# A four-layer decoder on one core: unread products of TensorE while outputs are fetched, masked heads' keys made in head mixing, loads between stores in the paged attention

## The chip, the core and the metric

The kernel runs on one core of a Trainium2 chip: TensorE (PE) for matrix products, VectorE (DVE), ScalarE (ACT) and GpSimd (POOL) for the rest, and SyncE (SP) that issues most transfers. The metric is the device time of one execution in microseconds (us). The granted clock of TensorE is told as a share of its full 2.4 GHz: 1.00 is 2.4 GHz and 0.50 is 1.2 GHz.

## What is computed

x has 2 x 1024 tokens of width 256. Twelve sublayers follow each other, each as `x = layernorm(x + f(x))`. Those that the change touches, cut to what matters:

```python
# L0_attn: heads of one token attend to each other (16 heads of 16)
kv = (x @ Wdown + bdown) @ Wup + bup                   # latent of 64
att = softmax(einsum('bthd,btgd->bthg', rope(q), rope(k)) / 4)
x = layernorm(x + einsum('bthg,btgd->bthd', att, v) @ Wout + bout)
# L0_xattn: 16 masked heads over a context of 77 rows
k, v = ctx @ Wk.T + bk, ctx @ Wv.T + bv
scores = where(mask == 0, -1e9, q @ k.T / 4)
x = layernorm(x + softmax(scores) @ v @ Wo.T + bo)
# L0_ffn: a gated FFN with ternary weights and 8-bit rows
# L1_attn: attention by pages of 64 rows, 16 heads of 16
k = rope((x @ w_down) @ wk_up)
scores = where(page(key) <= page(query), q @ k.T / 4, min)
# L1_ffn: 8 experts, the one with the highest score;  L2_ffn: 8 experts, two of them, with a capacity
x = layernorm(x + sum_over_choices(gate * expert(x)))
```

The others are a context attention (L1_xattn), a gated linear attention (L2_attn), a self-attention on the context (L2_xattn), a causal linear attention (L3_attn), L3_xattn and a quantized FFN (L3_ffn).

## The kernel before

Each sublayer is a stage, a function with one program for each engine; the engines agree by semaphores. x stays in SBUF twice, token-major (`x_tok`) and turned (`xT`), in 16 tiles of 128 tokens. The order on each engine is the order in which the program is written.

**Head mixing** (`head_mixing_stage`, line 593). SP loads x in pieces of 512 tokens (`CW`), then the next stage's weights (`early`). PE makes for each 512 tokens the latents (L675, `latents`), and for each tile the queries (L683, L686) and the keys and values (L690, `front`). DVE multiplies each query head with each key head (L805; half of it is on POOL, L870), sums (L814), weighs the values (L824) and norms (L833). PE sums the weighted values (L697, `mix`), turns them (L707) and projects (L715). `k` counts steps over the tiles; in step k PE works on `mix(k - 1)`, then `turn`, `front(k + 3)`, `project` and the layer norm's turned tiles (`tail.turn`, L3034). POOL adds the output bias to x in four pieces (L880). PE's first wait is for the weights (`loaded`), ACT's too; ACT's first Activation is behind the first latents.

**Masked heads** (`masked_heads_stage`, line 890). PE first makes K and V of the 77 context rows (L944, L948), DVE makes from them `kz` (L1085), `v` (L1088) and from the mask `fill` (L1090, L1092). Then, for each tile: queries (L959), ACT's copy `qT` (L1041), scores (L970), on DVE the masked scores (L1101), their maximum (L1104), the difference (L1106) and the sum (L1112). POOL adds the bias to x at the start (L1134).

**Paged attention** (`paged_attention_stage`, line 150). Queries and keys are split in bf16 parts; a part goes to DRAM and from there to the stacks Q and K of three slots. For each of the two sequences b there are four rounds r (r = 0, 1 the queries of two groups of heads, r = 2, 3 the keys). A round ends in ACT's casts (L274, L276), POOL's differences (L311, L314), DVE's L298, L300 and L304, and SP's store of two DMAs (L224). ACT may write the parts of round r only when the store of round r - 2 has landed (`stored[r % 2]`, L273). `load(slot)` issues 12 DMAs (L199): 6 for Q, 6 for K. SP's queue takes its DMAs in order:

```python
for b in range(B):
    for r in range(NR):
        sp.wait_ge(part_done[2], b * NR + r + 1)
        for g in range(2): sp.dma_start(parts_dram..., parts...)
        if b == 0 and r >= 2:
            for slot in range(2 * r - 4, min(2 * r - 2, SLOTS)):
                sp.wait_ge(stored[slot // 2], 16 * NR)
                load(sp, slot)
```

Behind it, DVE takes the row maxima (L527) of the first unit; SP puts their negatives into Q (L378), and PE makes the scores (L451).

**Experts** (`sparse_experts_stage`, line 1560). Behind the last expert's down product (L1667) the rows are gathered from DRAM (L1611). `weigh(1)` on PE multiplies the gathered rows with the gates and adds x (L1686, L1687); DVE takes the layer norm's sums from it (L2980). `keep_busy(nc, core, bank, n)` (line 2916) writes n products `ident @ zero` of 128x256 into a bank that nobody reads; in f32 the profile counts each product as two instructions.

## Time and profile before

| what | us |
|---|---|
| three runs: median (lowest to highest) | 2747.84 (2745.88 to 2752.18) |
| the profiled execution's own time | 2748.86 |
| its span, first to last instruction | 2747.1 |
| PE busy | 2432.6 (89%) |
| DVE busy | 1438.9 (52%) |
| ACT busy | 946.2 (34%) |
| POOL busy | 494.6 (18%) |
| mean granted clock | 0.937 |

| stretch of the trace | stage |
|---|---|
| 0 to 249.8 | head mixing |
| 249.8 to 375 | masked heads |
| to 494 | ternary FFN |
| 496 to 900 | paged attention |
| to 1214 | context attention, routing, top-1 experts |
| 1215 to 1685 | gated linear attention |
| to 2166 | second context attention, routing, top-2 experts |
| to 2747 | causal linear attention, context attention, FFN |

The stretches' rows give, for each engine, its busy time and its number of instructions. All times in the rows are from the span's start. A row of the timeline reads: start, duration, engine, line, operation, what it writes <- what it reads, shapes, number of instructions, and in brackets the time for which the engine stood idle before it and what ended that. Neighbouring instructions of the same kind are one row.

### The profile page before, as it was taken

To read this page: it belongs to the slowest core of one execution; us is meant where nothing else is said; L and a number is where in the kernel's file an instruction comes from. 1 tells how busy PE (TensorE), PEld (TensorE's weight loads), DVE (VectorE), ACT (ScalarE), POOL (GpSimd) and SP (SyncE) were. 2 spreads that over 40 slices of the span, in tenths; PEclk is the share of its full clock that TensorE was granted. 3 is DMA by queue.
4 is the path that set the end of the run, shared out by engine and by line. 5 is a ranking of instruction groups with operands and counts; after the bars stand their busy time and mean duration, and the time that the engine had idled before them with its cause. 6 is when DMAs were issued, how large, how long until landed. Compare 5 with 4: busy or idle time off the path is not lost. (4 is left out here: it accounts for less than half of the span.)

```text
span 2747.1 us, 36310 instructions
## 1 busy us (share of the span) xinstructions
PE 2432.6 (89%) x14259; PEld 1686.0 (61%) x14259; DVE 1438.9 (52%) x2474; ACT 946.2 (34%) x1799; POOL 494.6 (18%) x422
## 2 busy tenths in 40 slices
PE   6986767778889879979999998889999799999888
PEld 3665654422224768856667667757776577777764
DVE  7996979367773421036564653651110455455543
ACT  3443657225554213234442431311111322122132
POOL 3442320220001124310100011122221311001010
PEclk8998989969999979999999999779999899999999
DMA  3003100373420046622322230322231300000000
GB/s 113 1 1 122 48 32 1 58 145 50 69 44 26 5 173 226 226 89 89 93 71 65 67 98 0 104 58 101 77 90 56 103 18 18 12 18 12 1 33 31
DMA packets 77659, 181.47 MB, mean 66 GB/s; under 512 B 16935, under 2 KB 41128, under 8 KB 71945
## 3 DMA queue, kind: packets, MB, share of 16 engines
q1 hardware_dynamic: 64596, 126.74, 16.7%
q0 software_dynamic: 10368, 50.01, 5.3%
q10 hardware_dynamic: 2542, 2.62, 0.3%
q8 instruction: 103, 1.69, 0.3%
q14 instruction: 50, 0.41, 0.0%
HBM read 149.51 MB, written 25.43 MB: 64 GB/s over the span
## 5 line engine op out<-in xcount | busy, mean ns | idle before, releaser
L1655 PE MATMUL L_ffn_h_ps<-L_ffn_xgT,L_ffn_w 128*128 128x512 f32 (+2 forms) x992 | 231.9, 390 | 4.0 <-DVE L_ffn_xgT L1738 2.3
L1667 PE MATMUL L_ffn_y_ps<-L_ffn_w,L_ffn_h 128*128 128x256 f32 x1008 | 222.5, 380 | 4.8 <-issue 3.9
L1713 ACT ACTIVATE L_ffn_h<-L_ffn_h_ps,L_ffn_w 128x640 f32<-128x640 f32 (+2 forms) x184 | 101.6, 553 | 346.1 <-PE L_ffn_h_ps L1655 335.0
L527 DVE TENSOR_REDUCE L_attn_neg<-L_attn_Y 128x1 f32<-128x512 f32 (+3 forms) x304 | 187.4, 657 | 55.8 <-PE L_attn_Y L400 54.4
L1667 PEld LDWEIGHTS L_ffn_y_ps<-L_ffn_w,L_ffn_h 128*128 128x128 f32 x1008 | 189.9, 190 | 32.9 <-issue 8.3
L1655 PEld LDWEIGHTS L_ffn_h_ps<-L_ffn_xgT,L_ffn_w 128*128 128x128 f32 x992 | 153.8, 192 | 81.5 <-issue 66.8
L497 ACT ACTIVATE L_attn_room<-L_attn_Y 128x1024 f32<-128x1024 f32 (+1 forms) x192 | 147.4, 812 | 81.1 <-PE L_attn_Y L451 80.5
L400 PE MATMUL L_attn_Y<-L_attn_K,L_attn_Q 104*128 104x512 bf16 (+3 forms) x384 | 119.6, 363 | 44.9 <-DVE L_attn_neg L527 35.9
L1747 DVE TENSOR_TENSOR L_ffn_yg<-L_ffn_y_ps,L_ffn_w 128x256 f32<-128x256 f32 x63 | 26.7, 425 | 223.5 <-PE L_ffn_y_ps L1667 223.5
L1738 DVE COPY L_ffn_xgT<-L_ffn_t_ps 128x256 f32<-128x256 f32 x63 | 24.5, 421 | 212.1 <-PE L_ffn_t_ps L1642 211.7
L1788 POOL DMA_INDIRECT token_outputs<-L_ffn_yg,puts x63 | 61.8, 982 | 324.5 <-DVE L_ffn_yg L1747 324.5
L2362 PE MATMUL L_attn_X<-xT,L_attn_w 128*128 128x512 f32 x256 | 113.2, 595 | 0.0
L2362 PE MATMUL L_attn_X<-xT,L_attn_first_w 128*128 128x512 f32 x256 | 112.8, 593 | 0.0
L400 PEld LDWEIGHTS L_attn_Y<-L_attn_K,L_attn_Q 104*128 104x128 bf16 x384 | 33.8, 100 | 118.2 <-DVE L_attn_neg L527 105.0
L2910 POOL TENSOR_TENSOR L_attn_prod<-L_attn_k_sum,L_attn_qs 128x1024 f32<-128x1024 f32 x16 | 37.7, 2356 | 346.7 <-DVE L_attn_qs L2884 346.7
L451 PE MATMUL L_attn_Y<-L_attn_Q,L_attn_K 107*128 107x512 bf16 (+3 forms) x384 | 96.8, 338 | 2.0 <-ACT L_attn_room L497 1.9
L2588 POOL TENSOR_TENSOR L_attn_sq_sum<-L_attn_sq_sum,L_attn_sq 128x1024 f32<-128x1024 f32 x14 | 33.0, 2356 | 331.3 <-ACT L_attn_sq L2465 331.3
L2447 ACT ACTIVATE L_attn_bc<-L_attn_bc 128x1024 f32<-128x1024 f32 x32 | 33.8, 1057 | 169.7 <-DVE L_attn_bc L2540 169.7
L697 PE MATMUL L_attn_pv_ps<-L_attn_mixed,ident 128*128 128x256 f32 x256 | 64.8, 417 | 29.1 <-DVE L_attn_mixed L824 29.1
L870 POOL TENSOR_TENSOR L_attn_v_all<-L_attn_q,L_attn_kv 128x2048 f32<-128x2048 f32 x15 | 67.5, 4501 | 121.4 <-DVE L_attn_mixed L824 47.8
L436 PE MATMUL L_attn_Y<-L_attn_room,L_attn_v_all 128*32 128x512 f32 (+3 forms) x768 | 83.1, 511 | 0.0
L2362 PEld LDWEIGHTS L_attn_X<-xT,L_attn_w 128*128 128x128 f32 x256 | 47.9, 192 | 53.9 <-issue 53.9
(577 smaller groups left out, 5099.3 us busy)
## 6 DMA issues: line engine op xcount, KB each, us to landing
L_ffn_w<-in_L_ffn_w SPq DMA_DIRECT2D x8, 2180.0 KB
L_attn_bc<-decays SPq DMA_DIRECT2D x32, 512.0 KB, 6.1
L_attn_bp<-decays SPq DMA_DIRECT2D x32, 256.0 KB, 7.0
L_attn_Q<-L_attn_q_parts SPq DMA_DIRECT2D x48, 128.0 KB, 4.7
L_attn_K<-L_attn_k_parts SPq DMA_DIRECT2D x48, 128.0 KB, 7.6
L_attn_first_w<-in_L_attn_w SPq DMA_DIRECT2D x8, 640.0 KB
L_attn_w<-in_L_attn_w SPq DMA_DIRECT2D x8, 640.0 KB, 3.8
L_attn_v_all<-zero SPq DMA_DIRECT2D x1, 4096.0 KB, 22.5
```

Of the source, the lines that this page charges most:

```text
L400: mm = nc.tensor.matmul(R[n % 2][:, u * wdt:(u + 1) * wdt], Q[0:KM, par, j0 + u, tt * P:(tt + 1) * P], K[0:KM, par, j0 + u, c * CW:c * CW ...
L436: mm = nc.tensor.matmul(O[32 * j:32 * j + 32, lo:CW], v_all[:, it, gt, 32 * j:32 * j + 32], probs[:, (2 * n + j // 2) % 4, j % 2, lo:CW], ...
L451: mm = nc.tensor.matmul(S[e % 2][:, j % 2, lo:CW], K[0:KS, par, j, gt * P:(gt + 1) * P], Q[0:KS, par, j, tc * CW + lo:(tc + 1) * CW], star ...
L497: nc.scalar.activation(probs[:, e % 4, :, lo:CW], S[e % 2][:, :, lo:CW], ACT.Exp, scale=SCALE).then_inc(exp_done, 1)
L527: nc.vector.tensor_reduce(neg[:, c, j0:j0 + heads, tt], R[n % 2][:, 0:heads * width(tt, c)].rearrange("p (h k) -> p h k", h=heads), X_AXIS ...
L697: mm = nc.tensor.matmul(pv_ps[n % 2][:, 0:D], core.ident[:], mixed[n % 2][:, g, :, :].rearrange("p h d -> p (h d)"), start=g == 0, stop=g ...
L870: nc.gpsimd.tensor_tensor(prod[n % 2][:, h, :, :], q[n % 2][:, h, :].unsqueeze(2).broadcast_to([P, HALF, H, DH]), keys(n).unsqueeze(1).bro ...
L1655: ins = nc.tensor.matmul(h_ps[f % 2][:, lo // CW, 0:hi - lo], w1[g % NB][:, kt, f * P:(f + 1) * P], xgT[u][:, kt, lo:hi], start=kt == 0, s ...
L1667: ins = nc.tensor.matmul(y_ps[k % 2][:], h[:, f, t * P:(t + 1) * P], w2[g % NB][:, f, :], start=f == 0, stop=f == FT - 1)
L1713: nc.scalar.activation(h[:, f, 0:n], h_ps[f % 2][:].rearrange("p c n -> p (c n)")[:, 0:n], func, bias=b1[g % NB][:, f:f + 1]).then_inc(sem ...
L1788: nc.gpsimd.indirect_dma_start(core.outputs, at, yg[g % 2][:, t, :], None).then_inc(y_stored[g % 2], 16)
L2362: ins = nc.tensor.matmul(x[:, c * CW:(c + 1) * CW], w[1 - par][:, kt, r, :], xT[:, kt, b * T + c * CW:b * T + (c + 1) * CW], start=kt == 0 ...
```

## The change

Five parts.

- Head mixing, start: PE issues seven products of zeros (128x256) ahead of its wait for the weights; ACT runs one Exp on a single column ahead of its own wait; the latents come in pieces of 128, 384, 512, 512 and 512 tokens, so that the first tile needs only the first.
- Head mixing, end: the masked heads' K and V are multiplied at k = 13 on PE (`made.products`) and `fill`, `kz` and `v` made at k = 16 on DVE (`made.make`); the same work goes from the start of the masked heads, with the waits for it.
- Ternary FFN: `xq1`, `hr1` and `hqT` lie in buffers that the masked heads have left. No instruction is added or moved.
- Paged attention: loads between the second sequence's stores, not the first's.
- Both expert stages: twelve unread products ahead of `weigh(1)`.

```diff
@@ projections_on_sync
                 for r in range(NR):
-
+                    if b == 1 and r < SLOTS:
+                        sp.wait_ge(stored[r // 2], 16 * NR)
+                        load(sp, r)
                     sp.wait_ge(part_done[2], b * NR + r + 1)
...
-                    if b == 0 and r >= 2:
-                        for slot in range(2 * r - 4, min(2 * r - 2, SLOTS)):
-                            sp.wait_ge(stored[slot // 2], 16 * NR)
-                            load(sp, slot)
@@ head_mixing_stage
+        PIECES = (0, P, CW, 2 * CW, 3 * CW, N)
+        piece = lambda n: 0 if n == 0 else n // 4 + 1
+        warm = m.sb("warm", [P, 1])
...
         def _(pe):
+            for _ in range(7):
+                nc.tensor.matmul(y_ps[:, 0, :], core.zero[:, 0:P], core.zero[:], start=True, stop=True)
             pe.wait_ge(loaded, ALL)
...
-                pe.wait_ge(core.x_loaded, 16 * (c + 1))
+                lo, hi = PIECES[c:c + 2]
+                pe.wait_ge(core.x_loaded, 16 * max(1, c))
...
-                    mm = nc.tensor.matmul(lat_ps[0:LAT, :], wdown[:, kt, :], xT[:, kt, c * CW:(c + 1) * CW], start=kt == 0, stop=kt == KT - 1)
+                    mm = nc.tensor.matmul(lat_ps[0:LAT, 0:hi - lo], wdown[:, kt, :], xT[:, kt, lo:hi], start=kt == 0, stop=kt == KT - 1)
...
             latents(0)
             front(0)
+            latents(1)
             front(1)
...
                 if k >= 2:
                     project(k - 2)
+                if k == NT_ - 3:
+                    pe.wait_ge(q_ready, NT_)
+                    pe.wait_ge(kv_ready, NT_)
+                    made.products(pe, lat_ps[:], (q_ps[:], kv_ps[:]))
                 for g in TURNS.get(k, ()):
                     tail.turn(pe, g)
...
+            nc.scalar.activation(warm[:], core.one[:], ACT.Exp)
             act.wait_ge(loaded, ALL)
...
                     tail.add(dve, (k - 4) // 2)
+                if k == NT_:
+                    made.make(dve, lat_ps[:], (q_ps[:], kv_ps[:]))
@@ masked_heads_stage, on PE and DVE
-            for mt in range(KT):
-                for kt in range(KT):
-                    nc.tensor.matmul(S_ps[:, mt, 0:B * S2], wk[:, kt, mt * P:(mt + 1) * P], ctxT[:, kt, :],
-                                     start=kt == 0, stop=kt == KT - 1)
...
-            pe.wait_ge(k_ready, 1)
             scores(0)
-            pe.wait_ge(v_ready, 1)
...
-            dve.wait_ge(kv_mm, 1)
-            for mt in range(KT):
-                for h in range(2):
-                    last = nc.vector.tensor_scalar(kz[:, mt, :, h, :], ...
...
@@ the experts' stage, on PE
+            keep_busy(nc, core, banks[3][:, 0:2 * P], 12)
             weigh(1)
@@ new
+class MaskedKeys:
...
+    def products(self, pe, k_bank, v_banks):
+        pe.wait_ge(self.early.loaded, self.early.all)
...
+                nc.tensor.matmul(k_bank[:, mt * B * S2:(mt + 1) * B * S2], w["kw"][:, kt, mt * P:(mt + 1) * P], w["ctxT"][:, kt, :],
+                                 start=kt == 0, stop=kt == KT - 1)
...
+                mm = nc.tensor.matmul(v_banks[b][0:S2, :], w["ctxT"][:, kt, b * S2:(b + 1) * S2], w["vw"][:, kt, :],
+                                      start=kt == 0, stop=kt == KT - 1)
+        mm.then_inc(self.multiplied, 1)
+    def make(self, dve, k_bank, v_banks):
+        dve.wait_ge(self.early.loaded, self.early.all)
+        nc.vector.tensor_scalar(self.fill[:], w["mask"][:], 0.0, None, ALU.not_equal).then_inc(self.keep_set, 1)
+        dve.wait_ge(self.multiplied, 1)
...
```

How the change moves instructions, at three places. SP in the paged attention, before: the stores (`q_parts`, `k_parts`, L224) and the loads (`Q`, `K`, L199), six DMAs of each for a slot.

```order
L224 DMA L_attn_q_parts<-L_attn_parts 64x3x1024 x4
L224 DMA L_attn_k_parts<-L_attn_parts 64x3x1024 x2
L199 DMA L_attn_Q<-L_attn_q_parts 16x4x1024 x6
L199 DMA L_attn_K<-L_attn_k_parts 16x4x1024 x6
L199 DMA L_attn_Q<-L_attn_q_parts 16x4x1024 x6
L199 DMA L_attn_K<-L_attn_k_parts 16x4x1024 x6
L224 DMA L_attn_k_parts<-L_attn_parts 64x3x1024 x2
L199 DMA L_attn_Q<-L_attn_q_parts 16x4x1024 x6
L199 DMA L_attn_K<-L_attn_k_parts 16x4x1024 x6
L224 DMA L_attn_q_parts<-L_attn_parts 64x3x1024 x4
L224 DMA L_attn_k_parts<-L_attn_parts 64x3x1024 x4
```

The same place now (the lines of the changed kernel are other ones: L226 is the store).

```order
L226 DMA L_attn_q_parts<-L_attn_parts 64x3x1024 x4
L226 DMA L_attn_k_parts<-L_attn_parts 64x3x1024 x4
L199 DMA L_attn_Q<-L_attn_q_parts 16x4x1024 x6
L199 DMA L_attn_K<-L_attn_k_parts 16x4x1024 x6
L226 DMA L_attn_q_parts<-L_attn_parts 64x3x1024 x2
L199 DMA L_attn_Q<-L_attn_q_parts 16x4x1024 x6
L199 DMA L_attn_K<-L_attn_k_parts 16x4x1024 x6
L226 DMA L_attn_q_parts<-L_attn_parts 64x3x1024 x2
L199 DMA L_attn_Q<-L_attn_q_parts 16x4x1024 x6
L199 DMA L_attn_K<-L_attn_k_parts 16x4x1024 x6
L226 DMA L_attn_k_parts<-L_attn_parts 64x3x1024 x4
```

The first sequence's four stores stand ahead of every load, and each of the second sequence's first three has a slot's loads ahead of it. PE at the start of head mixing, now (before, the first row was missing and the latents were one row of 64x512):

```order
L670 MATMUL L_attn_y_ps<-zero 128x256 x7
L679 MATMUL L_attn_lat_ps<-xT,L_attn_wdown 64x128 x2
L687 MATMUL L_attn_q_ps<-L_attn_wq,xT 128x256 x2
L690 MATMUL L_attn_q_ps<-L_attn_bq,L_attn_lat 128x256
L694 MATMUL L_attn_kv_ps<-L_attn_wup,L_attn_lat 128x512
L679 MATMUL L_attn_lat_ps<-xT,L_attn_wdown 64x384 x2
```

The first keys and values (L694) have a quarter of the latents ahead of them. PE near the end of head mixing, now: the three rows with `L_xattn_` operands are new there.

```order
L701 MATMUL L_attn_pv_ps<-L_attn_mixed,ident 128x256 x16
L711 MATMUL L_attn_oT_ps<-ident,L_attn_o 128x128 x2
L719 MATMUL L_attn_y_ps<-L_attn_wout,L_attn_oT 128x256 x2
L3078 MATMUL L_attn_lat_ps<-L_xattn_ctxT,L_xattn_kw 128x154 x4
L3082 MATMUL L_attn_q_ps<-L_xattn_vw,L_xattn_ctxT 77x512 x2
L3082 MATMUL L_attn_kv_ps<-L_xattn_vw,L_xattn_ctxT 77x512 x2
L3023 MATMUL L_attn_x_ps<-ident,x_tok 128x128 x4
L701 MATMUL L_attn_pv_ps<-L_attn_room,ident 128x256 x16
```

They stand between the projection of tile 11 and the turned tiles (`x_ps`), ahead of the sum `pv_ps` of tile 13.

## Rows read from the trace of the kernel before

**Rows 1.** Stretch; busy us of PE, PEld, DVE, ACT, POOL; clock, DMA share, GB/s

```profile
1258.00:1685.00 427.00, 411.19 (x2635) 287.96 (x2634) 237.78 (x321) 155.53 (x146) 38.41 (x19) 0.99 0.26 74
```

**Rows 2.** Timeline of PE and DVE, start of head mixing

```profile
8.15 3.67 PE L675 MATMUL L_attn_lat_ps<-xT,L_attn_wdown 128*64 128x512 f32 x4 [8.15 <-DMA L_attn_bdown<-in_L_attn_bdown]
...
13.94 1.12 PE L690 MATMUL L_attn_kv_ps<-L_attn_wup,L_attn_lat 65*128 65x512 f32 x2
14.90 1.03 PE L683 MATMUL L_attn_q_ps<-L_attn_wq,xT 128*128 128x256 f32 x4
...
16.49 1.13 PE L690 MATMUL L_attn_kv_ps<-L_attn_wup,L_attn_lat 65*128 65x512 f32 x2
...
15.83 4.43 DVE L805 TENSOR_TENSOR L_attn_v_all<-L_attn_q,L_attn_kv 128x4096 f32<-128x4096 f32 x1 [11.76 <-ACT L_attn_kv L762]
```

**Rows 3.** Timeline, end of head mixing, PE and DVE

```profile
209.88 8.83 PE L697 MATMUL L_attn_pv_ps<-L_attn_room,ident 128*128 128x256 f32 x32 [2.28 <-DVE L_attn_room L824]
...
221.70 1.13 PE L715 MATMUL L_attn_y_ps<-L_attn_wout,L_attn_oT 128*128 128x256 f32 x4 [2.77 <-ACT L_attn_oT L784]
...
232.43 7.07 PE L697 MATMUL L_attn_pv_ps<-L_attn_room,ident 128*128 128x256 f32 x32
...
239.54 0.42 DVE L833 TENSOR_TENSOR L_attn_o<-L_attn_pv_ps,L_attn_den 128x256 f32<-128x256 f32 x1 [5.59 <-PE L_attn_pv_ps L697]
```

**Rows 4.** Timeline of POOL, PE and DVE, masked heads from their start

```profile
249.86 9.25 POOL L1134 TENSOR_TENSOR x_tok<-x_tok,L_xattn_ob 128x1024 f32<-128x1024 f32 x4 [3.05 <-POOLq L57]
...
257.23 1.48 DVE L1085 TENSOR_SCALAR L_xattn_kz<-L_xattn_S_ps,L_xattn_kb,L_xattn_pair 128x154 f32<-128x154 f32 x4 [9.65 <-PE L_xattn_t_ps L948]
...
259.87 0.81 PE L970 MATMUL L_xattn_S_ps<-L_xattn_kz,L_xattn_qT 32*128 32x154 f32 x16
...
261.41 1.44 DVE L1101 TENSOR_TENSOR L_xattn_s<-L_xattn_S_ps,L_xattn_fill 128x1232 f32<-128x1232 f32 x1
...
274.87 1.91 PE L959 MATMUL L_xattn_q_ps<-xT,L_xattn_qw 128*128 128x128 f32 x8
```

**Rows 5.** Timeline of POOL and DVE, head mixing: a DVE product beside POOL, and alone

```profile
24.88 2.34 POOL L880 TENSOR_TENSOR x_tok<-x_tok,L_attn_bout 128x1024 f32<-128x1024 f32 x1
...
25.08 4.29 DVE L805 TENSOR_TENSOR L_attn_v_all<-L_attn_q,L_attn_kv 128x2048 f32<-128x2048 f32 x1
...
203.12 2.28 DVE L805 TENSOR_TENSOR L_attn_v_all<-L_attn_q,L_attn_kv 128x2048 f32<-128x2048 f32 x1
```

**Rows 6.** Timeline of POOL, SP's queue, ACT, DVE and PE, start of the paged attention

```profile
539.46 2.13 POOL L314 TENSOR_TENSOR L_attn_parts<-L_attn_oT,L_attn_parts 128x1024 bf16<-128x1024 f32 x1 [1.16 <-ACT L_attn_parts L276]
...
552.19 1.24 SPq L224 DMA_DIRECT2D L_attn_k_parts<-L_attn_parts  x2
...
558.62 1.23 DVE L304 TENSOR_TENSOR L_attn_oT<-L_attn_oT 128x1024 f32<-128x1024 f32 x1
...
567.51 1.04 ACT L274 CAST L_attn_parts<-L_attn_oT 128x1024 bf16<-128x1024 f32 x1 [11.95 <-DMA L_attn_k_parts<-L_attn_parts]
...
574.13 1.23 DVE L298 TENSOR_TENSOR L_attn_oT<-L_attn_Y,L_attn_room 128x1024 f32<-128x1024 f32 x1 [10.70 <-POOL L_attn_parts L314]
...
577.73 25.53 DVE L527 TENSOR_REDUCE L_attn_neg<-L_attn_Y 128x4 f32<-128x512 f32 x38
...
611.23 1.06 PE L451 MATMUL L_attn_Y<-L_attn_Q,L_attn_K 107*128 107x512 bf16 x2
```

**Rows 7.** Timeline of PE and DVE, behind the last expert: top-1, then top-2

```profile
1193.21 1.19 PE L1686 MATMUL L_ffn_y_ps<-L_ffn_got,L_ffn_gates 128*128 128x256 f32 x2 [6.86 <-DMA L_ffn_got<-token_outputs]
...
1197.01 0.76 DVE L2980 BATCH_NORM_STATS2 L_ffn_tail_stats<-L_ffn_y_ps 128x6 f32<-128x256 f32 x2 [2.67 <-PE L_ffn_y_ps L1687]
...
2141.73 2.04 PE L1686 MATMUL L_ffn_y_ps<-L_ffn_got,L_ffn_gates 128*128 128x256 f32 x4 [8.59 <-DMA L_ffn_got<-token_outputs]
...
2146.68 0.76 DVE L2980 BATCH_NORM_STATS2 L_ffn_tail_stats<-L_ffn_y_ps 128x6 f32<-128x256 f32 x2 [3.64 <-PE L_ffn_y_ps L1687]
```

**Rows 8.** Busy time by stretch, top-2 stage: the clock in the gap

```profile
2136.00:2137.00 1.00, 0.00 (x0) 0.00 (x0) 0.00 (x0) 0.00 (x0) 0.00 (x0) 0.50 0.00 0
```

More of the change, by code:

```diff
@@ L590, in _, with head_mixing_stage @@
                 tail.root(pool, g)
[L593 removed]
+def head_mixing_stage(nc, core, early, room, made):
     A = core.A
@@ L731, in _ @@
                     if (k + 3) % 4 == 0:
-                        latents((k + 3) // 4)
+                        latents(piece(k + 3))
                     front(k + 3)
@@ L765, in _ @@
             queries_keys_values(0)
+            latents(1)
             queries_keys_values(1)
@@ L786, in _ @@
                     if (k + 3) % 4 == 0:
-                        latents((k + 3) // 4)
+                        latents(piece(k + 3))
                     queries_keys_values(k + 3)
@@ L887, in _, with masked_heads_stage @@
                     tail.shift(pool, g)
-def masked_heads_stage(nc, core, early, bit, values):
+def masked_heads_stage(nc, core, early, bit, values, made):
     A = core.A
@@ L902, in masked_heads_stage @@
     with Mem(nc, name) as m:
[L903 to L904 removed]
+        wq, bq, wo, bo = [early.tiles[n] for n in ("qw", "qb", "ow", "ob")]
         junk = m.sb("junk", [P, KT * 1024])
[L906 to L908 removed]
+        fill, kz, v = made.fill, made.kz, made.v
         qT = [m.sb(f"qT{u}", [P, KT, P]) for u in range(2)]
@@ L1148, with bit_ffn_stage @@
 ROUND = 1.5 * 2.0 ** 23
-def bit_ffn_stage(nc, core, weights, values, following):
+def bit_ffn_stage(nc, core, weights, values, following, made):
     F = 1024
@@ L1168, in bit_ffn_stage @@
         xr = [m.sb(f"xr{u}", [P, QT, D]) for u in range(2)]
-        xq = [m.sb(f"xq{u}", [P, QT, D], BF16) for u in range(2)]
+        xq = [m.sb("xq0", [P, QT, D], BF16), made.early.tiles["qw"][:].rearrange("p k n -> p (k n)").bitcast(BF16).rearrange("p (t d) -> p t d", d=D)]
         xqT = m.sb("xqT", [P, KT, N], BF16)
@@ L1172, in bit_ffn_stage @@
         h = [m.sb(f"h{u}", [P, F]) for u in range(2)]
-        hr = [m.sb(f"hr{u}", [P, F]) for u in range(2)]
-        hqT = [m.sb(f"hqT{u}", [P, FT, P], BF16) for u in range(2)]
+        hr = [m.sb("hr0", [P, F]), made.fill[:].rearrange("p n k -> p (n k)")[:, 0:F]]
+        turned = made.early.tiles["vw"][:].rearrange("p k n -> p (k n)").bitcast(BF16)
+        hqT = [turned[:, u * F:(u + 1) * F].rearrange("p (f n) -> p f n", n=P) for u in range(2)]
         hmax, h127, hscale, sh = [m.sb(n, [P, NT_]) for n in ("hmax", "h127", "hscale", "sh")]
@@ L3507, in build @@
     masked, bit = masked_early(nc, early, A), BitWeights(nc, early, A)
+    made = MaskedKeys(nc, early, masked)
     late, ffn = ExitStack(), []
@@ L3514, in build @@
     sublayers = [
-        lambda: head_mixing_stage(nc, core, (masked,), (paged[0], paged[2])),
-        lambda: masked_heads_stage(nc, core, masked, bit, paged[0]),
-        lambda: bit_ffn_stage(nc, core, bit, paged[0], paged[3]),
+        lambda: head_mixing_stage(nc, core, (masked,), (paged[0], paged[2]), made),
+        lambda: masked_heads_stage(nc, core, masked, bit, paged[0], made),
+        lambda: bit_ffn_stage(nc, core, bit, paged[0], paged[3], made),
         lambda: paged_attention_stage(nc, core, contexts[0], paged_held, paged),
```

48 lines of the change are left out of this document (24 added, 24 removed).

## The prediction

> **What bounds the kernel now.** I read the table of stretches first, to see which engine each stage hangs on, and then the timeline at each place that the change touches, asking there only which wait ends last. TensorE (PE) is the bound in the long middle: in the gated attention it is busy 411 of 427 us at a granted clock of 0.99 [rows 1]. The change touches nothing there. Its places lie elsewhere: the start of head mixing, where VectorE (DVE) is idle until 15.83 [rows 2] and then saturated; the end of the same stage [rows 3]; the start of the masked heads, where DVE idles 9.65 [rows 4]; the first stores and loads of the paged attention [rows 6]; and the gap behind the last expert of two stages [rows 7]. I count a saving only where the waiting engine bounds the work behind it. The sum is made against the profiled execution, 2748.86, which is 1.0 above the median of the three runs shown.
>
> **1. Start of head mixing: -3.7.** PE waits for the first weights until 8.15. The latents of 512 tokens then take 3.67 for 4 instructions, and the first K/V product (L690) starts at 13.94 [rows 2]. Now the first piece has 128 of the 512 columns, and Exp's table is loaded on ScalarE (ACT) before the weights land, not behind the latents. A matmul of 512 columns at 0.92 is 1.2 GHz. The seven unread ones (14 instructions of 256 columns, so half of that, 0.46 at most) take 6.4 at most from about 1.9, where the stage begins, to 8.3: they cost the path 0 to 0.2. They raise the clock: before, L683 took 1.03 for four at 14.90, the 2.4 GHz rate, some 6.7 after PE's first work; PE will now have worked 6 by 8.15. At the warm rate the piece takes about 0.5, and from the end of latents to L690 I take the second tile's step, 16.49 - 14.90 = 1.59. So L690 starts at 8.15 + 0.5 + 1.59 = 10.24, 3.7 sooner, and DVE with it, at 12.1. The other end: clock still at 1.2 GHz, everything doubled, L690 at 12.3, a gain of 1.6. L805 and its successors keep DVE full from then on, so the shift stays.
>
> **2. Keys made in head mixing: 0.** The 8 K products and 8 V products (L944, L948; 7.2 from the start of the masked heads to kz at 257.23 [rows 4], at a clock that was low for most of it; between half of that and all, I take 5.0) now stand on PE before turn(2). PE was idle 2.28 there, until 209.88, so mix(13) starts some 2.7 later. But that mix took 8.83, where the same 32 instructions take 7.07 warm, since the clock had just fallen in the idle gap [rows 3]; with the gap filled most of 1.8 comes back. What is left is below 1.5, and the next product of PE (L715) waited 2.77 for ACT in any case [rows 3]. On DVE, kz, v and fill are 4.2 (257.23 to 261.41 [rows 4]); they land in the idle 5.59 before 239.54 [rows 3], in which DVE waits for PE. Cover gone, the two would cost 1.5 and 4.2; that is the bad end of this term.
>
> **3. Start of the masked heads: -5.2.** Before: products, kz from 257.23, softmax of the first tile (L1101) at 261.41, and DVE nearly full behind it. After, at 249.87: queries(0) cold 1.91, queries(1) 1.91, scores twice 0.81 = 1.6 since the clock is low [rows 4], and 0.8 for ACT's copy between the queries and the hand-overs: L1101 at about 256.2, so -5.2. If the clock is up the queries take half and L1101 starts at 253.9 (-7.5).
> A row speaks against the full gain. In head mixing DVE's L805 takes 2.28 alone, but 4.29 when GpSimd's (POOL) L880 started 0.2 before it [rows 5]: that product waited for POOL. In the masked heads POOL adds the bias (L1134) from 249.86 to 259.11 [rows 4], before under an idle DVE, now under softmax. L1106 has two inputs in SBUF like L805 and starts 2.9 after L1101: at 259.1 by my sum, just clear of it, and at 256.8 if the start is warm, when it would wait up to 2.3. So the gain is 5.2 both ways; a half-warm start gives at least 4.
> The Trainium skill, SBUF — State Buffer, section "Who interferes with whom", states this as a rule: a DVE instruction with two SBUF inputs and a GpSimd instruction that reads SBUF exclude each other for the whole instruction, while one with a single SBUF input is free. By that rule L1101 and L1104 are untouched and the term is capped near 5.3; without it the warm end would stand at 7.5. [rows 5] agree with the rule.
>
> **4. Paged attention: -7.5.** Before, the last store of b=0 is issued at 552.19, though POOL's part (L314) is ready at 541.6; two waits and 24 loads stand ahead of it. It lands at 567.4: there ACT's cast L274 ends an idle 11.95. Behind the cast come POOL, DVE's L298 at 574.13 after 10.70 idle, and the row maxima L527 at 577.73, 38 of them back to back, on which the -max rows and the first scores (L451, 611.23) wait [rows 6]. DVE is full with them, so what comes sooner there stays. Now that store is issued at about 541.6, as soon as POOL has its part, and is not behind any load. The cast then waits for its own input, L304's result at 559.9 [rows 6], and is ready 7.6 sooner. L527 starts at 570.2 and L451 at 603.7. What is moved: 12 + 12 + 12 loads go behind one store each. Each 128 KB load took about 1.0 of the full queue (24 of them and the store: 541 to 567.4), a store of 384 KB x 2 about 3 to 5. load(0) is issued by 549 and lands by 559; b=1's first store goes behind it (part ready 557.8), lands at 563; load(1) lands by 575; store r=1 (566.5) by 577; load(2) by 588; the last two stores by 592. Slot 0 is wanted at 570.2, slot 1 some 26 later, the table of the -max rows at 600: all are met, the tightest by 8. SP's own waits: load(1) stands behind part r=0, and nothing waits for it before 590. Bounds: 0 (another transfer takes the store's place) and -7.6.
>
> **5. Experts: -2.0 and -1.0.** After the last down of the top-1 stage PE idles 6.86 until the gathered rows land (1193.21), and weigh(1) then runs at 1.2 GHz until DVE's L2980 at 1197.01, 3.8 later, DVE having waited 2.67 [rows 7]. Twelve unread products (24 instructions, 0.22 each warm) fill 5.2 of the gap; 1.7 stay idle. The clock then should still be up, and weigh(1) takes half: DVE starts 1.9 to 2.1 sooner: -2.0. In the top-2 stage the gap is 8.59; the clock was down at 2136, 2.9 after PE stopped at 2133.15 [rows 8]. The 12 end at 2138.4, 3.3 before the rows land at 2141.73, so the clock may have fallen again or not. Warm, the 4.95 to L2980 (2146.68) would halve: -2.3; cold, 0. I take -1.0. Worse than 0 only if the 12 themselves ran at 1.2 GHz (10.5): +1.9 in top-2.
> Buffers in other places (bit FFN): 0; no instruction moves.
>
> **Sum.** 3.7 + 0 + 5.2 + 7.5 + 2.0 + 1.0 = 19.4: 2748.86 - 19.4 = 2729.5, and 1.0 less for the median: 2728.5, say 2729. About 0.2% (5.5) can be told from no change.
>
> **Rivals.**
> (a) *The store is no longer late, but something else is.* In the paged start the shared queue is full from 541 to 578; if load(0) or the -max rows come late, or PE at 1.2 GHz (it is at the low level there) holds the maxima back, term 4 is 0: 2736.5. For it: the full queue. Against: the slack of 8. Chance 0.13.
>
> (b) *The clock isn't where I put it.* A rise or fall that comes a few us later takes 2.1 off term 1, 2 off term 5, and POOL's lock 1.2 off term 3: 2734. Chance 0.13. By the Trainium skill's rule named above (SBUF — State Buffer, "Who interferes with whom") the 1.2 for L1106 is due in full whenever the start is half warm.
>
> (c) *More than I count*: a warm masked start without a meeting of L1106 and POOL (2.3) and a warm top-2 (1.3): 2725. Chance 0.06. By the skill's rule only the 1.3 of it could come.
>
> (d) *The change doesn't do what it says*: making the keys in head mixing pushes its tail back by the bad end of term 2 (5.7), the start stays cold (1.6) and the store's wait moves on: 1.6 + 5.2 + 2.0 - 5.7 = 3.1, 2745. Chance 0.03.
>
> (e) *Slower*: the clock steps change phase, since all work after 250 comes at other times. If a stage that runs at 0.99 [rows 1] fell to 1.2 GHz, each us there would cost half: the sum is eaten after 39 us at the low level, and 50 give 2754. For it: the clock does fall inside other stages. Against: PE is 96% busy there and its pauses do not change. Chance 0.03.
>
> **How the numbers follow.** The forecast as summed has 0.62, with its own range 2723 to 2734. To hold 8 in 10, the range takes in (a), (b) and (c): 2720 to 2740. Faster by over 0.2%: 0.62 + 0.13 + 0.13 + 0.06, less 0.01 for the far end of (a), = 0.93. The same: (d), that 0.01 and a third of (e), 0.05. Slower by over 0.2%: the rest of (e), 0.02.
>
> **What would show it.** DVE's first L805 at about 12.1; PE without idle before mix(13) and DVE's L833 near 239.5 less 3.7; L1101 6.3 after the masked stage begins, against 11.5; ACT's L274 ending its wait on DVE, not on a transfer; L527 and L451 7.5 closer to the stage's start; L2980 1.9 closer to the last down in top-1. The prediction is wrong if head mixing does not end 3.7 sooner, if L451 waits for a transfer, or if a stage untouched by the change has another length or clock.

## The result, and the profile after

The changed kernel took 2736.27 us in the median of five runs (2733.05 to 2748.39), the kernel before 2747.84 in five (2745.88 to 2754.05); the ratio is 0.9943, with a 95% interval of 0.9922 to 0.9964 (the quotient of these two medians, 0.9958, lies inside it). The forecast was 2729, with 2720 to 2740 as its range. The profiled execution has a span of 2734.5 where the one before had 2747.1: 12.6 less, at the same mean clock of 0.937. The page of the changed kernel, parts 1 and 2:

```profile
PE 2450.2 (90%) x14317; PEld 1700.9 (62%) x14325; DVE 1439.3 (53%) x2475; ACT 948.8 (35%) x1801; POOL 497.8 (18%) x422
...
PEclk8998989979999889999999998779999999999999
```

PE has 58 instructions and 17.6 us more than before: 16.5 of it are the unread products (5.77 and twice 5.34). The other engines do the same work, so the 12.6 are waits, and the pace at which PE ran. Place by place, first the start of head mixing (timeline of PE and DVE; lines are those of the changed kernel: L679 is the latents, L694 the keys and values, L817 DVE's first product):

```profile
1.85 5.77 PE L670 MATMUL L_attn_y_ps<-zero 128*128 128x256 f32 x14 [1.85 <-PEq L118]
...
8.00 0.65 PE L679 MATMUL L_attn_lat_ps<-xT,L_attn_wdown 128*64 128x128 f32 x4 [0.38 <-DMA L_attn_bdown<-in_L_attn_bdown]
...
10.27 1.12 PE L694 MATMUL L_attn_kv_ps<-L_attn_wup,L_attn_lat 65*128 65x512 f32 x2
...
12.16 4.43 DVE L817 TENSOR_TENSOR L_attn_v_all<-L_attn_q,L_attn_kv 128x4096 f32<-128x4096 f32 x1 [8.09 <-ACT L_attn_kv L773]
```

DVE starts at 12.16, where the forecast had 12.1 and the kernel before 15.83 [rows 2]. Next the end of head mixing (timeline of ACT, DVE and PE):

```profile
207.28 0.59 ACT L3030 COPY xT<-L_attn_x_ps 128x512 f32<-128x512 f32 x1 [5.15 <-PE L_attn_x_ps L3023]
...
212.60 4.42 DVE L836 TENSOR_TENSOR L_attn_mixed<-L_attn_sc,L_attn_kv 128x4096 f32<-128x4096 f32 x1 [0.76 <-ACT L_attn_sc L785]
...
217.58 1.14 PE L719 MATMUL L_attn_y_ps<-L_attn_wout,L_attn_oT 128*128 128x256 f32 x4 [3.20 <-ACT L_attn_oT L796]
...
219.49 8.30 PE L701 MATMUL L_attn_pv_ps<-L_attn_mixed,ident 128*128 128x256 f32 x32
...
237.07 0.42 DVE L845 TENSOR_TENSOR L_attn_o<-L_attn_pv_ps,L_attn_den 128x256 f32<-128x256 f32 x1 [1.63 <-PE L_attn_pv_ps L701]
```

The last row stood at 239.54 before [rows 3]: only 2.5 of the 3.7 are left. ACT stood idle 5.15 for the turned tiles that now come behind the keys' products, its exponents came later, and DVE waited 0.76 for them, which it did not do before. Then PE idled 3.20, its clock fell, and the sum of tile 14 took 8.30, not 7.07.

The shift was not 3.7 all the way to that place. DVE's weighing of tile 13 (L824, L836) and its norm of tile 14 (L833, L845) in both traces (timeline of DVE, before and then after):

```profile
205.32 4.42 DVE L824 TENSOR_TENSOR L_attn_room<-L_attn_sc,L_attn_kv 128x4096 f32<-128x4096 f32 x1
...
230.30 0.43 DVE L833 TENSOR_TENSOR L_attn_o<-L_attn_pv_ps,L_attn_den 128x256 f32<-128x256 f32 x1 [4.29 <-PE L_attn_pv_ps L697]
...
200.56 4.42 DVE L836 TENSOR_TENSOR L_attn_room<-L_attn_sc,L_attn_kv 128x4096 f32<-128x4096 f32 x1
...
227.83 0.42 DVE L845 TENSOR_TENSOR L_attn_o<-L_attn_pv_ps,L_attn_den 128x256 f32<-128x256 f32 x1 [5.87 <-PE L_attn_pv_ps L701]
```

The weighing comes 4.76 sooner. From it to the norm it is 24.98 before and 27.27 now: the end of the stage gives back 2.29. The 1.2 by which the whole stage falls short of 3.67 is this loss less a gain of 1.1 in the middle.

The start of the masked heads (timeline of POOL and DVE):

```profile
247.39 9.27 POOL L1121 TENSOR_TENSOR x_tok<-x_tok,L_xattn_ob 128x1024 f32<-128x1024 f32 x4 [3.04 <-POOLq L57]
...
253.79 1.44 DVE L1088 TENSOR_TENSOR L_xattn_s<-L_xattn_S_ps,L_xattn_fill 128x1232 f32<-128x1232 f32 x1 [8.67 <-PE L_xattn_S_ps L971]
...
256.74 1.44 DVE L1093 TENSOR_TENSOR L_xattn_s<-L_xattn_s,L_xattn_mx 128x1232 f32<-128x1232 f32 x1
```

The softmax begins 6.4 after the stage, against 11.55 before [rows 4]; L1093 starts as POOL ends (256.66) and takes its usual 1.44. The start of the paged attention (timeline of ACT, DVE and PE):

```profile
552.03 1.05 ACT L272 CAST L_attn_parts<-L_attn_oT 128x1024 bf16<-128x1024 f32 x1 [4.31 <-DVE L_attn_oT L302]
...
562.27 25.51 DVE L525 TENSOR_REDUCE L_attn_neg<-L_attn_Y 128x4 f32<-128x512 f32 x38
...
595.75 1.06 PE L449 MATMUL L_attn_Y<-L_attn_Q,L_attn_K 107*128 107x512 bf16 x2
```

The cast waits for its own input and no longer for a transfer. The maxima start 15.46 sooner than in [rows 6], the scores 15.48 sooner; 7.85 of that had been gained by 537.99, where DVE's first L296 of the second sequence starts (545.84 before). Last, the experts (timeline of PE and DVE, top-1 and top-2):

```profile
1181.27 0.67 PE L1674 MATMUL L_ffn_y_ps<-L_ffn_got,L_ffn_gates 128*128 128x256 f32 x2 [1.55 <-DMA L_ffn_got<-token_outputs]
...
1183.27 0.76 DVE L2969 BATCH_NORM_STATS2 L_ffn_tail_stats<-L_ffn_y_ps 128x6 f32<-128x256 f32 x2 [0.90 <-PE L_ffn_y_ps L1675]
...
2129.16 1.20 PE L1674 MATMUL L_ffn_y_ps<-L_ffn_got,L_ffn_gates 128*128 128x256 f32 x4 [3.28 <-DMA L_ffn_got<-token_outputs]
...
2133.71 0.76 DVE L2969 BATCH_NORM_STATS2 L_ffn_tail_stats<-L_ffn_y_ps 128x6 f32<-128x256 f32 x2 [3.15 <-PE L_ffn_y_ps L1675]
```

From the rows' arrival to DVE's sums it is 2.0 instead of 3.8 in top-1, and still 4.55 of 4.95 in top-2 [rows 7]. Counted from the last down product (DVE's last L1747, in lines of before) the gains are 1.92 and 0.53. These local gains, 3.67 - 1.2 + 5.15 + 7.6 + 1.92 + 0.53, are 17.7. The other 5.1 went where nothing was changed. Busy time by stretch: first from DVE's first token sum behind the paged attention (L2968) to the routing scores, called the context stretch below, before and after; then the first 44 to 46 us of the gated attention, before and after:

```profile
869.90:973.00 103.10, 94.09 (x508) 84.09 (x507) 46.02 (x131) 21.87 (x45) 14.79 (x25) 0.91 0.04 9
...
1215.70:1260.00 44.30, 38.51 (x184) 22.54 (x178) 27.43 (x38) 20.30 (x21) 0.00 (x0) 0.96 0.38 116
```

```profile
855.40:961.80 106.40, 97.44 (x508) 86.59 (x507) 46.01 (x131) 21.93 (x45) 14.79 (x25) 0.88 0.04 9
...
1200.80:1247.00 46.20, 41.74 (x190) 23.97 (x184) 28.12 (x39) 20.59 (x21) 0.00 (x0) 0.89 0.35 111
```

The first has the same 508 PE instructions, 3.3 us more of PE time and a clock of 0.88 for 0.91. The second pair does not end at the same instruction (184 and 190 of PE); counted from DVE's L2481 to its first L2555 (lines of before), it is 46.9 before and 48.5 after. What had to be found out was whether that loss belongs to the change.

### The profile page after: what moved, and what is told of

It is laid out like the page before. It is cut to its first block and busy times, and to the rows that moved or that the text cites. A ratio compares the mean times of both kernels' runs of the same rounds, so it can differ in the third digit from the quotient of the medians.

```text
span 2734.5 us, 36437 instructions
## 1 busy us (share of the span) xinstructions
PE 2450.2 (90%) x14317; PEld 1700.9 (62%) x14325; DVE 1439.3 (53%) x2475; ACT 948.8 (35%) x1801; POOL 497.8 (18%) x422
## 3 DMA queue, kind: packets, MB, share of 16 engines
q8 instruction: 103, 1.69, 0.3%
## 5 line engine op out<-in xcount | busy, mean ns | idle before, releaser
L2351 PEld LDWEIGHTS L_attn_X<-xT,L_attn_first_w 128*128 128x128 f32 x256 | 47.7, 192 | 55.2 <-issue 55.2
```

The lines of the kernel that those rows point to most:

```text
L2351: ins = nc.tensor.matmul(x[:, c * CW:(c + 1) * CW], w[1 - par][:, kt, r, :], xT[:, kt, b * T + c * CW:b * T + (c + 1) * CW], start=kt == 0 ...
```

## The experiments

Each of the first four has one part of the change on the kernel before. Theory P says that the untouched stages follow the places at which the clock happens to be low; theory S that the change, above all its loads, does something to them. The expectations take the gated attention's start as 44.3 and 46.2, from the unequal windows above. Because single parts are worth less than the runs differ (the runs of the kernel before reach from 2738.26 to 2763.64), each is judged by its traces' rows, and the ratio stands beside it.

**e1, the loads alone.** Edit: in `projections_on_sync`

```diff
+                    if b == 1 and r < SLOTS:
+                        sp.wait_ge(stored[r // 2], 16 * NR)
+                        load(sp, r)
...
-                    if b == 0 and r >= 2:
...
```

> The kernel before with the change to the paged attention's loads alone. Theory P (phase): the 5.3 us that the changed kernel lost in stages which no part touches (context attention with routing 103.1 -> 106.4, start of the gated attention 44.3 -> 46.2) come from the low-clock stretches falling in other places, and which part moved the work does not matter. Theory S (structure): they belong to this part, because the paged attention now leaves the queue or TensorE in another state. Both expect ScalarE's cast L274 to wait for VectorE and not for a transfer, and the row maxima L527 to begin 8 to 9 us sooner than 577.7. S expects the context stage at 106.4 and the gated attention's start at 46.2 again, so a time 3 us below before. P expects any length between 103 and 107 for the context stage, tied to its mean granted clock (0.91 at 103.1, 0.88 at 106.4), and a time 5 to 9 us below before.

Measured: ratio 0.9986 (0.9965 to 1.0008), median 2742.77 beside 2746.79. The cast waits for DVE; the maxima begin at 569.10, 8.6 sooner, of which 1.0 was there ahead of this part (its first L298 of the second sequence stands at 544.83 for 545.84). The context stretch took 101.6, less than in any other trace, which speaks against S. But in this trace the rest of the paged attention took 5.6 longer than in the trace of before, and the span was 2749.4. One trace can't tell whether a gain reaches the end, but all thirteen tell that the part does not lengthen the rest: from the first maximum to the token sums it is 293.1 in the mean of the eight traces with this part (291.2 to 297.8) and 293.1 in the mean of the five without (290.5 to 295.7).

**e2, the start alone.** Edit: the seven unread products, the early Exp and `PIECES`, without `made`.

> The kernel before with the change to the start of head mixing alone (seven unread products, early table load, latents in pieces). VectorE's first product L805 at 12.2 instead of 15.83 and the end of head mixing 3.7 sooner, since nothing is put on TensorE near the end. If the 1.2 us that the changed kernel gave back by the end of that stage belongs to the start (clock at other places), it shows here too: end 2.5 sooner. Theory S: context stage 103.1, gated attention's start 44.3, time 3.7 below before. Theory P: these two lengths can move by up to 3 and 2 with their granted clock though no part near them is in the kernel; time 0 to 7 below before.

Measured: ratio 0.9989 (0.9968 to 1.001), median 2746.75. DVE's first product is at 12.31, the weighing of tile 13 at 202.40, 2.9 sooner than before. At the end of head mixing, though, nothing is left of it, where 3.7 or 2.5 had been expected (timeline of PE, and of DVE, e2):

```profile
218.78 2.07 PE L721 MATMUL L_attn_y_ps<-L_attn_wout,L_attn_oT 128*128 128x256 f32 x4 [2.77 <-ACT L_attn_oT L794]
...
221.50 8.77 PE L703 MATMUL L_attn_pv_ps<-L_attn_mixed,ident 128*128 128x256 f32 x32
...
230.31 0.42 DVE L843 TENSOR_TENSOR L_attn_o<-L_attn_pv_ps,L_attn_den 128x256 f32<-128x256 f32 x1 [7.21 <-PE L_attn_pv_ps L703]
```

The last row starts at 230.30 before. PE had idled 2.77 and ran at 1.2 GHz from 218 to 225 (granted clock 0.51). Before, PE idled the same 2.77 at this place [rows 3], and the clock stayed at 1.00. The sum of tile 13 took 8.83 in both traces and costs nothing there, since PE has to wait for ACT behind it; in e2 the sum of tile 14 ran low too, and for that one DVE and everything behind it wait. The context stretch is 103.0, as S has it and P allows.

**e3, the keys alone.** Edit: `made.products`, `made.make` and the buffers that they need, without the rest.

> The kernel before with the masked heads' keys made in head mixing alone (and the ternary FFN's buffers in their new places, which it needs). If the products of keys on TensorE cost the tail of head mixing, VectorE's L833 for tile 14 (before at 230.30) comes 1 to 1.5 later; if not, at 230.3. The masked heads' first softmax L1101 comes 5 to 8 sooner than 261.41 less that. Theory S: context stage 103.1 and gated attention's start 44.3, time 5 below before. Theory P: lengths move with the clock, time 2 to 9 below before.

Measured: ratio 0.9989 (0.997 to 1.0007), median 2748.35. Timeline of DVE, e3:

```profile
218.06 4.42 DVE L828 TENSOR_TENSOR L_attn_mixed<-L_attn_sc,L_attn_kv 128x4096 f32<-128x4096 f32 x1 [0.72 <-ACT L_attn_sc L777]
...
231.59 0.42 DVE L837 TENSOR_TENSOR L_attn_o<-L_attn_pv_ps,L_attn_den 128x256 f32<-128x256 f32 x1 [4.17 <-PE L_attn_pv_ps L697]
```

The wait for ACT is there without any change at the start, so it belongs to the keys. Tile 14 comes 1.29 later than before (230.30), but 0.74 of that was already there when tile 13 was weighed (206.06 for 205.32), 0.34 of it since the first product (16.17 for 15.83). From that weighing to tile 14 it is 25.54, against 24.98 before: the keys' own share is 0.56, with the clock up. The softmax starts at 257.95, 3.5 sooner in all, and 6.4 behind the stage's start.

**e4, the experts alone.** Edit: `keep_busy(nc, core, banks[3][:, 0:2 * P], 12)` ahead of `weigh(1)`.

> The kernel before with the unread products in the two expert stages alone. Everything ahead of 1186 as before within 0.3, context stage included, if the clock's places depend only on the work ahead; if they also differ from run to run, the context stage moves here although nothing ahead of it was changed. VectorE's L2980 in the top-1 stage 1.6 to 2.0 sooner than 1197.01 and TensorE's weigh(1) at 2.4 GHz; in the top-2 stage 0 to 1 sooner than 2146.68 (0.5 in the changed kernel, where the clock fell again in the 3.3 us left idle). Time 2 to 3 below before.

Measured: ratio 0.9992 (0.9972 to 1.0012), median 2746.43. L2980 comes 8.72 after DVE's last L1747 in top-1, 10.61 before. In top-2 it comes 14.12 after it, 13.50 before, so here nothing was gained: the gathered rows landed later (PE's gap was 9.73, not 8.59), and weigh(1) had 4.43 to the sums for 4.95. The telling part is ahead of 1186, where this kernel is the kernel before, instruction for instruction: from its first maximum to the token sums the paged attention took 295.7 where the trace of before has 292.2. So 3.5 us between two traces need no change at all.

**e5, the changed kernel again.**

> The changed kernel once more, for more runs and a second trace. Theory P (phase): its untouched stages come out otherwise than in the first trace (context attention with routing 106.4, start of the gated attention 46.2 there; any length of 103 to 107 and 44 to 47 here), and with them the total moves by up to 5 us; its mean over twelve runs is 12 to 17 below before, since the local gains (3.7 at the start, 5 at the masked heads, 8 at the paged attention, 1.9 and 0.5 at the experts, less 1.2 at the end of head mixing: 18) are real. Theory S (structure): the same two lengths again within 0.3, and 11 to 12 below before.

Measured: six runs, median 2728.83 (2724.61 to 2733.08), ratio 0.9922 (0.99 to 0.9944). That is 21 below before by the ratio, more than either theory had. The context stretch by busy time, e5:

```profile
853.40:956.60 103.20, 94.20 (x508) 84.00 (x506) 45.98 (x131) 21.87 (x45) 14.82 (x25) 0.91 0.04 9
```

103.2 at 0.91, in the very kernel that had 106.4 at 0.88: S is wrong and P is right on this stretch. The gated attention's start, counted from L2481 to the first L2555 in instructions of before, took 50.1 here and 48.5 in the first trace. It is 46.9 in the trace of before and 46.4 to 50.6 over all thirteen traces, so the trace of before stands near the short end. The four kernels with a single part have 48.1 to 50.6, and the 46.4 is that of e8, which has all parts but one: the length goes with no part.

**e6, the keys' products in two places.** Edit, on the changed kernel:

```diff
+                if k == NT_ - 2:
+                    made.keys(pe, lat_ps[:])
+                    made.values(pe, q_ps[:], 0)
                 if k >= 2:
                     project(k - 2)
                 if k == NT_ - 3:
...
-                    made.products(pe, lat_ps[:], (q_ps[:], kv_ps[:]))
+                    made.values(pe, kv_ps[:], 1)
```

> The changed kernel with the keys' products split: the values of the second sequence stay at k = 13 on TensorE, the keys and the values of the first go one step later, ahead of the projection of tile 12, where TensorE idled 3.20. If the tail of head mixing lost its 1.2 because ScalarE's turned-tile copy and with it the exponents of tile 14 waited for the products (VectorE idle 0.76 in front of L836 at 212.60) and because the clock fell in the 3.20 gap (the sum of tile 14 took 8.30 instead of 7.07), then here VectorE does not wait there, the sum takes 7.07, and L833/L845 of tile 14 comes 1 to 1.5 sooner than 227.83, with everything in head mixing ahead of it as in the changed kernel. If it is the mere amount of work on TensorE, nothing changes. Time 0 to 2 below the changed kernel, which the timing can't tell.

Measured: ratio 0.9916 (0.9893 to 0.9939), median 2728.03. Timeline of DVE and PE, e6:

```profile
212.53 4.42 DVE L839 TENSOR_TENSOR L_attn_mixed<-L_attn_sc,L_attn_kv 128x4096 f32<-128x4096 f32 x1
...
219.21 7.07 PE L701 MATMUL L_attn_pv_ps<-L_attn_mixed,ident 128*128 128x256 f32 x32
...
226.32 0.42 DVE L848 TENSOR_TENSOR L_attn_o<-L_attn_pv_ps,L_attn_den 128x256 f32<-128x256 f32 x1 [4.29 <-PE L_attn_pv_ps L701]
```

DVE no longer waits, the sum takes 7.07, and tile 14 comes at 226.32, 1.5 sooner than in the changed kernel, with the same work on PE. From the weighing of tile 13 to tile 14 it is 24.98, as before the change, so all 2.29 are back. The wait for ACT is gone by the edit; the clock did not fall either, behind a gap of 1.69 instead of 3.20; it did not in e9 and e10, which have the same edit. The context stretch was 106.3 at 0.88 in this trace: the long form comes back in another kernel.

**e7, other counts of unread products.** Edit: the loop of seven removed, and

```diff
-            keep_busy(nc, core, banks[3][:, 0:2 * P], 12)
+            keep_busy(nc, core, banks[3][:, 0:2 * P], 8 if choices == 1 else 18)
```

> The changed kernel with other counts of unread products: none at the start of head mixing, 8 instead of 12 in the top-1 stage, 18 in the top-2 stage. The forecast's view: at the start TensorE is at 1.2 GHz, so VectorE's first product comes at 13.0 to 14.2 instead of 12.16. In top-1 the 8 end 3.3 us ahead of the gathered rows, the clock falls as it did in top-2 with 12, and L2980 comes 1.2 to 1.9 later behind the last down product than in the changed kernel. In top-2 the 18 end within 1 us of the gathered rows, weigh(1) runs at 2.4 GHz, and L2980 comes about 1.8 sooner. Rival view: unread products do nothing for the clock that the real ones don't do, and all three places stay as in the changed kernel within 0.3. Net time 0 to 1.5 above the changed kernel.

Measured: ratio 0.9927 (0.9904 to 0.9951), median 2731.56. Timeline of DVE, e7:

```profile
15.12 4.42 DVE L815 TENSOR_TENSOR L_attn_v_all<-L_attn_q,L_attn_kv 128x4096 f32<-128x4096 f32 x1 [11.06 <-ACT L_attn_kv L771]
...
1181.27 0.76 DVE L2967 BATCH_NORM_STATS2 L_ffn_tail_stats<-L_ffn_y_ps 128x6 f32<-128x256 f32 x2 [2.33 <-PE L_ffn_y_ps L1673]
...
2129.71 0.76 DVE L2967 BATCH_NORM_STATS2 L_ffn_tail_stats<-L_ffn_y_ps 128x6 f32<-128x256 f32 x2 [1.46 <-PE L_ffn_y_ps L1673]
```

Without the unread products DVE starts at 15.12, later than the 14.2 at which the expectation ended: they carry 3.0 of the 3.7, and the pieces with the early table only 0.7 without them. With 8 in top-1, L2967 comes 10.21 after the last down product's L1734, 8.69 with 12: all but 0.4 of the gain is gone. With 18 in top-2 it comes 11.35 after, 12.97 with 12 and 13.50 with none. Over the traces it is 12.9 to 13.1 with 12 (but 14.12 in e4) and 13.0 to 13.5 with none, so that 12 do anything there is not clear of the spread; what 18 do is. The rival view falls at all three places.

**e8, the changed kernel without the loads.** Edit: `projections_on_sync` as before.

> The changed kernel without its part on the paged attention's loads. Both views: ScalarE's cast L274 waits 12 for the late store again and the row maxima begin 8 to 9 later than in the changed kernel, counted from the stage's start. If the gain there reaches the end of the program, the mean over twelve runs lies 7 to 9 above the changed kernel of the same batch; if the paged attention gives it back later (e1 kept only 2 of its 7.6 at the end of the stage), 0 to 3 above.

Measured: median 2738.2 (11 runs) beside 2728.83 of e5 on the same chip, ratio to before 0.9954 (0.9937 to 0.9971). Timeline of ACT, e8:

```profile
564.54 1.04 ACT L274 CAST L_attn_parts<-L_attn_oT 128x1024 bf16<-128x1024 f32 x1 [15.27 <-DMA L_attn_k_parts<-L_attn_parts]
```

In the means (2737.9 and 2728.8) the loads are worth 9.1, give or take some 2 by the spread of the runs. So the gain does reach the end. It is larger here than between before and e1, as is the wait: 15.27, and from DVE's first L298 of the second sequence to the maxima 35.2 against 24.3 with the part in place, 10.9; between before and e1 it was 31.9 against 24.3. This stretch is 24.3 in all eight traces with the part and 31.0, 31.9, 31.9, 35.2 and 35.5 in the five without: what the part takes away differs from trace to trace, what it leaves does not.

**e9, both repairs**: e6 with 18 products in top-2.

> The changed kernel with the two repairs that the runs point to: the keys' products split over two steps, and 18 instead of 12 unread products in the top-2 stage. From the traces: head mixing 1.4 shorter, L2980 in top-2 1.8 to 2.1 sooner behind the last down product than with 12. Mean over the runs 2 to 4 below the changed kernel of the same batch; if phase takes it all, 0.

**e10, and a warm start of the masked heads**: e9 with

```diff
+                if g == AFTER[-1]:
+                    keep_busy(nc, core, q_ps[:, 0:D], 7)
                 tail.turn(pe, g)
```

> e9_both with seven more unread products ahead of the last turned tiles of head mixing, where TensorE idled 3.30 and the clock then fell, so that the masked heads start at 2.4 GHz. By the queue of TensorE alone the first softmax comes 4.1 to 4.5 behind the start of GpSimd's L1121 (6.4 in the changed kernel). Port view, by the row of head mixing where VectorE's two-input product took 4.29 beside GpSimd and 2.28 alone: the softmax's two-input step L1093 then starts 7 behind the start of GpSimd's four adds (9.3 long), meets the last of them, and either takes up to 3.7 instead of 1.44 or starts as late as before, or GpSimd's add takes longer instead, if VectorE was first. Rival: no meeting, L1093 takes 1.44 and the masked heads end 2 sooner. Time 0 to 2 below e9.

**e11, the changed kernel a third time.**

> The changed kernel a third time, as the measure for the two above, on the same chip: 17 to 21 below before in the mean if the forecast's sum of 19.4 was right and the 11.6 of the first five runs was the draw of the clock; 10 to 14 if the first five were typical. Its untouched stages (context attention with routing, start of the gated attention) again with other lengths than 106.4 and 46.2 if they follow the clock.

Measured, on one chip with a before of 2753.47: e9 2728.96, ratio 0.9916 (0.99 to 0.9932); e10 2732.92, 0.9918 (0.9899 to 0.9938); e11 2736.75, 0.9931 (0.9912 to 0.9951). In the means e11 is 18.4 below before, inside the 17 to 21 expected if the forecast's sum was right. In e9 tile 14 comes 1.8 sooner than in the changed kernel's first trace and L2980 in top-2 11.6 after the last down product. The spread of the runs does not part e9 from e11 for certain; the rows do. One of e10's six runs took 6612.89, more than twice the others; it is in the median, left out of the ratio, and was not explained. Timeline of POOL and DVE, e10:

```profile
246.49 9.28 POOL L1126 TENSOR_TENSOR x_tok<-x_tok,L_xattn_ob 128x1024 f32<-128x1024 f32 x4 [3.04 <-POOLq L57]
...
251.98 1.44 DVE L1093 TENSOR_TENSOR L_xattn_s<-L_xattn_S_ps,L_xattn_fill 128x1232 f32<-128x1232 f32 x1 [7.76 <-PE L_xattn_S_ps L976]
...
254.93 2.15 DVE L1098 TENSOR_TENSOR L_xattn_s<-L_xattn_s,L_xattn_mx 128x1232 f32<-128x1232 f32 x1
```

The first softmax came 5.5 behind the stage's start, not 4.1 to 4.5: only queries(0) ran warm (1.13), queries(1) took 2.08 again. L1098, 1.44 in all other kernels, now starts 0.84 before POOL's last add ends (255.77) and takes 2.15. So the port view is right: DVE's two-input step stood until POOL was done. The Trainium skill, SBUF — State Buffer, section "Who interferes with whom", has this as its rule, that such a DVE instruction and a GpSimd instruction that reads SBUF lock each other out; the trace agrees, with 0.71 lost. The one-input L1093 at 251.98 ran beside the same adds in 1.44, as the rule also says. The context stretch of e11 was 103.1, so of three traces of the changed kernel one has the long form. The long form came in two of the seven traces of the changed kernel and of e6, e7, e9 and e10, and in none of the other six (101.6 to 103.3); whether the change makes it more frequent can't be told from so few.

## Why the prediction was right, and where it was off

**The start** (term 1, -3.7): measured -3.67, by the reasons given. Its other end was too kind: without the unread products the K/V product starts at 12.29, as put there, but itself takes 2.08 instead of 1.12, so that DVE's first product comes at 15.12, not 14.2. That the shift "stays" because DVE is full was wrong, already in the middle of the stage (timeline of PE and DVE, the sum of tile 4, before and then after):

```profile
92.93 7.14 PE L697 MATMUL L_attn_pv_ps<-L_attn_mixed,ident 128*128 128x256 f32 x32 [3.00 <-DVE L_attn_mixed L824]
...
105.80 0.69 DVE L2968 TENSOR_TENSOR x_tok<-L_attn_y_ps,x_tok 128x512 f32<-128x512 f32 x1 [0.82 <-PE L_attn_y_ps L715]
...
88.11 8.83 PE L701 MATMUL L_attn_pv_ps<-L_attn_mixed,ident 128*128 128x256 f32 x32 [3.00 <-DVE L_attn_mixed L836]
...
102.67 0.69 DVE L2957 TENSOR_TENSOR x_tok<-L_attn_y_ps,x_tok 128x512 f32<-128x512 f32 x1 [2.51 <-PE L_attn_y_ps L719]
```

Behind the same idle 3.00 the sum took 8.83 in one trace and 7.14 in the other, and DVE waited 2.51 for 0.82. By such places, and by which of DVE's product and POOL's bias add began first, the shift went from 3.67 over 4.8 and 2.9 to 4.76 at tile 13. The sums of tiles 14 and 15 are PE's, and DVE waits for them: a low clock there took back the last 2.9 in e2. Over the whole stage the three traces of the changed kernel lost 1.0 to 1.5 of their first 3.4 to 3.7.

**The keys** (term 2, 0). The step that failed: I looked for cover on PE and DVE and counted 2.7 of lateness on PE as covered, but not the queue of ACT, where the copy of the turned tiles stands ahead of tile 14's exponents, and DVE waits for these. By local distance, in us:

| traces | weighing of tile 13 to tile 14 | DVE's wait for ACT | sum of tile 14 |
|---|---|---|---|
| before, e1, e4 | 24.98 to 24.99 | none | 7.07 |
| keys at k = 13, clock up: e3, e5, e8 | 25.53 to 25.54 | 0.72 | 7.07 |
| keys at k = 13, clock low: after, e7, e11 | 27.18 to 27.27 | 0.73 to 0.76 | 8.30 to 8.40 |
| keys split: e6, e9, e10 | 24.98 to 24.99 | none | 7.07 |
| start alone, clock low: e2 | 27.91 | none | 8.77 |

So the missed queue costs 0.56, and the clock 1.7 more in three of the six traces with it. The idle gap ahead of that fall was 3.20 in the first trace and 3.12 in e11, and 3.12 in e3, e5 and e8 too, where the clock stayed up: its length alone does not decide. The +1.2 that stands in the sum of local gains for the end of head mixing is a net of this loss and of the gain in the middle. The make on DVE did hide in PE's sum, with 1.63 of idle left.

**The masked heads** (term 3, -5.2): -5.15. The clock was low, and L1093 cleared POOL by 0.1, as summed. The lock, of which only the row of head mixing spoke, was shown in e10. That the gain is "5.2 both ways" nearly holds: with queries(0) warm the first softmax came 0.9 sooner, but DVE's next masked scores 10.5 behind the stage's start (257.00) for 10.7 in the changed kernel (258.10), since the lock took 0.7 back.

**The paged attention** (term 4, -7.5): 31.9 to 24.3 from L298 to the maxima, -7.6, and 9.1 in the means of e8 against e5. No product of PE waited for one of the loads. That the late store can cost 10.9, as in e8, and not 7.6 was not seen.

**The experts** (term 5, -2.0 and -1.0): -1.92 and -0.53. In top-2 the clock was low during weigh(1) (0.63 in the mean) and the -0.53 is within what traces without unread products differ by; 18 products, against none, give -2.15, near the -2.3 that the forecast gave for a warm one.

**The sum.** 19.4 was forecast, 17.7 is the sum of the local gains, 12.6 the difference of the two spans, 11.6 that of the medians. Between 17.7 and 12.6 stands rival (b), but not where I put it: 3.4 in the context stretch and 1.6 at the start of the gated attention, stages that I had taken as fixed. Other untouched stretches moved by up to 1.2 either way and cancel to 0.1. The 3.4 are the clock's draw, since the same kernel has both lengths. For the 1.6 that is argued: the changed kernel's three traces have 48.5 to 50.1 and never the 46.9 of before, of which there is one trace, but no part goes with the length. That the first five runs still gave a median inside the range is partly luck: the loss that the range allowed for was put in other places. Over three comparisons the ratios are 0.9943, 0.9922 and 0.9931, which is 15.7, 21.4 and 19 us; 19.4 lies in the interval of each. Rival (e) did not come: the gated attention behind its start took 418.7 at 0.99, 418.2 at 1.00 before. What stays open is which idle gap decides the context stretch's 103 or 106: its clock was read, but no run tried to change it.

## What to carry to other kernels

When work is put into another engine's idle gap, follow each engine's queue behind it to the next consumer: here the gap was real, and 0.56 was lost two engines further on, over a copy in ScalarE's queue. A filler of unread products has to reach to the moment at which the real work starts: 12 were right for a gap of 6.9 and too few for one of 8.6, and 8 were worth nearly nothing. When a change shifts all later work, judge it by local distances in the trace and by many runs, since stretches that it does not touch move by up to 7 us from trace to trace (the paged attention from its first maximum to the token sums: 290.5 to 297.8). Take the distance from the last point ahead of the change: counted from the trace's start, e3's tile 14 is 1.29 late, and 0.56 of that is the change.
